# Turning the first attention's products round by head pairs, with attention weights turned by scaled identities

## The reference

```python
bias = jnp.full((n, n), NEG).at[diag, diag].set(0.0).at[dst, src].set(edge_weight)
q, k, v = jnp.split(x @ Wqkv.T + bqkv, 3, axis=-1)            # then 8 heads of 64 features
scores = jnp.einsum('hnd,hmd->hnm', q, k) / np.sqrt(HEAD_DIM) + bias[None]
attn = jax.nn.softmax(scores, axis=-1)
out = jnp.einsum('hnm,hmd->hnd', attn, v).transpose(1, 0, 2).reshape(n, EMBED_DIM)
h = layer_norm(x + out @ Wo.T + bo, g1, beta1)
h = layer_norm(h + (h @ W1.T + b1), g2, beta2)
```

## Time and profile before

| | us |
|---|---|
| median of three runs | 522.73 |
| profiled execution | 521.94 |
| its span | 519.9 |
| TensorE busy | 463.9 (89%) |
| VectorE busy | 323.7 (62%) |
| ScalarE busy | 181.5 (35%) |
| mean granted TensorE clock | 0.971 |

### The profile page before, as it was taken

The page is one execution under the profiler, slowest core; times in us unless marked ns, Lnnn a source line. Parts: engine busy times, 40 slices in busy tenths (PEclk is TensorE's granted clock), DMA queues, the critical chain, the costliest instruction groups (busy, mean ns, idle before and its releaser), DMA issues.

```text
span 519.9 us, 6791 instructions
## 1 busy us (share of the span) xinstructions
PE 463.9 (89%) x2153; PEld 274.4 (53%) x2153; DVE 323.7 (62%) x653; ACT 181.5 (35%) x352; POOL 151.0 (29%) x161
## 2 busy tenths in 40 slices
PE   6769999999689999998999999757898799998995
PEld 2422256665558998443444444545553587443442
DVE  7978989899968774787125200489998700267115
ACT  1259677665448762112101021242343232002010
POOL 5449034433350024132003500246633400003000
PEclk9988999999887999998999999899999999999998
DMA  7700000000044008152400020000002100000002
GB/s 256 264 2 0 1 1 2 2 1 2 2 149 177 1 2 314 57 196 82 141 0 0 5 77 0 0 1 0 1 1 90 73 1 0 1 0 0 0 1 81
DMA packets 13601, 25.80 MB, mean 50 GB/s; under 512 B 896, under 2 KB 1280, under 8 KB 13568
## 3 DMA queue, kind: packets, MB, share of 16 engines
q1 hardware_dynamic: 13568, 25.38, 14.1%
HBM read 24.33 MB, written 1.05 MB: 49 GB/s over the span
## 4 chain that ended last, share of the span: by engine, by line
PE 58%; DVE 32%; issue 4%; ACT 3%; DVEq 2%; DMA 0%; POOL 0%; POOLq 0%; SPq 0%; ACTq 0%
PE ring L1207 32%; PE banks L1376 5%; PE ring L1213 4%; DVE G L1158 4%; DVE G L1152 4%; DVE G L1169 4%; DVE HH L879 3%; PE ring L1476 3%; PE banks L1476 3%; PE banks L1316 2%; PE ring L1286 2%; DVE X L861 2%; DVE W_SD L905 2%; PE ring L1460 1%; DVE st L1024 1%
## 5 line engine op out<-in xcount | busy, mean ns | idle before, releaser
L1207 PE MATMUL ring<-G,WA 128*128 128x512 f32 x160 | 71.9, 605 | 3.1 <-ACT WA L562 2.5
L500 POOL TENSOR_TENSOR RB<-X,vec 128x512 f32<-128x512 f32 x16 | 21.1, 1328 | 148.1 <-DVE X L1049 110.1
L1207 PEld LDWEIGHTS ring<-G,WA 128*128 128x128 f32 x160 | 30.4, 194 | 39.5 <-issue 36.8
L470 POOL TENSOR_TENSOR A_SD<-A_SD,HH 128x128 f32 x64 | 32.0, 500 | 63.4 <-ACT HH L622 55.4
L1316 PE MATMUL banks<-RB,WB 128*128 128x128 f32 x256 | 45.6, 304 | 0.0
L1053 DVE TENSOR_TENSOR HH<-ring,RB 128x512 f32<-128x512 f32 x14 | 9.6, 686 | 53.1 <-PE ring L1207 53.1
L1152 DVE TENSOR_REDUCE G<-ring 128x256 f32<-128x2048 f32 x8 | 18.3, 2292 | 36.0 <-PE ring L1460 35.8
L576 ACT ACTIVATE sd<-mv,eps 128x1 f32<-128x1 f32 x32 | 9.4, 294 | 86.9 <-DVE mv L1029 86.9
L1316 PEld LDWEIGHTS banks<-RB,WB 128*128 128x128 f32 x256 | 37.1, 206 | 0.0
L562 ACT ACTIVATE WA<-ring 128x512 f32<-128x512 f32 x40 | 23.2, 591 | 35.6 <-PE ring L1213 35.6
L534 POOL TENSOR_TENSOR G<-G 128x1024 f32<-128x1024 f32 x7 | 16.5, 2358 | 59.9 <-ACT G L698 44.7
(11 more groups left out here) (195 smaller groups left out, 910.4 us busy)
## 6 DMA issues: line engine op xcount, KB each, us to landing
WA<-in_wqkv SPq DMA_DIRECT2D x2, 1024.0 KB, 8.5
WB<-in_wo SPq DMA_DIRECT2D x2, 1024.0 KB, 6.7
WC<-in_w SPq DMA_DIRECT2D x2, 1024.0 KB, 7.9
G<-in_w SPq DMA_DIRECT2D x1, 2048.0 KB, 10.4
G<-in_w SPq DMA_DIRECT2D x2, 1024.0 KB, 6.8
WA<-in_xT SPq DMA_DIRECT2D x4, 256.0 KB, 4.9
WA<-in_wqkv SPq DMA_DIRECT2D x4, 256.0 KB, 5.1
vec<-in_g SPq DMA_DIRECT2D x4, 256.0 KB, 7.9
```

The costliest lines, as they stand in the source:

```text
L470: pool.tensor_tensor(win, win, cnt_g[:, q, :, :], ALU.add).then_inc(group_added, 1)
L500: pool.tensor_tensor(out_, x_, vec[:, slot[vector], :], ALU.add).then_inc(resid_ready, 1)
L1207: last = nc.tensor.matmul(t[:, :], lhs(k), rhs_(k), start=(k == 0), stop=(k == n_k - 1))
```

## The change

- The products are turned round: the values (64 columns of one head) are the loaded tile, and the turned weights stream, 512 columns at once. The result is already turned, features by nodes. Two heads make a pair: one writes partitions 0 to 63 and the other partitions 64 to 127 of the same bank, so bank `j` holds heads 2j and 2j+1.
- The division by the row sums moves into the turning. Instead of `transpose`, an ordinary product streams a 128 by 128 diagonal matrix, which is the identity scaled by the inverse sums (`inverse_diag`, in `QB`). The diagonals of two heads fit. VectorE takes the inverse of the sums of a head and writes the diagonals of odd blocks, ScalarE those of even blocks, both in the turn before.
- Exponentials and row extremes run two heads ahead (`HEADS_AHEAD`), and `probsT` holds four heads.
- VectorE copies a finished pair to `outT` (in `W_SD`). The tile `OT` is gone. `Wo` is applied with the pairs as the outer loop: the four blocks are finished only in the last quarter.
- The load of `w12b` (1,024 KB, into `W_SD`) moves behind the last `WO`, and GpSimd's four residuals in `QB` behind the last `PT`.

```diff
+HEADS_AHEAD = 2
...
-    for b in range(NB):
-        add("OT", (b,), "A")
...
-        probsT = [XT, WA[:, 2, :, :]]
+        probsT = [XT, WA[:, 2, :, :], KB, HH]
+        outT = W_SD
+        inverse_diag = QB[:, 2:4, :].rearrange("p s (b n) -> p s b n", b=NB)
...
-            wait_full(sp, ("BD", NB - 1))
-            load("w12b", W_SD[:, :, :], blocks(a["w12"][:, D:2 * D]))
             wait_full(sp, ("PT", H - 1, NB - 1))
...
             load("wo2", WB[:, :, :], blocks(a["wo2"]))
+            load("w12b", W_SD[:, :, :], blocks(a["w12"][:, D:2 * D]))
...
+            wait_full(pool, ("PT", H - 1, NB - 1))
             for b in range(NB):
                 resid(QB[:, b, :], X[:, b, :], "be20")
...
+            def spread_inverse(h):                       # ScalarE
+                act.wait_ge(sums_inverted, NB + h)
+                if h >= 2:
+                    wait_full(act, ("PT", h - 2, NB - 1))
+                for b in range(0, NB, 2):
+                    act.activation(inverse_diag[:, h % 2, b, :], ident[:, :], ACT.Copy,
+                                   scale=inverse_sums[:, h * NB + b:h * NB + b + 1]).then_inc(diag_by_act, 1)
-            for b in range(NB):
-                exp0(0, b)
+            for h in range(HEADS_AHEAD):
+                for b in range(NB):
+                    exp0(h, b)
             for h in range(H):
                 for b in range(NB):
-                    if h + 1 < H:
-                        exp0(h + 1, b)
+                    if h + HEADS_AHEAD < H:
+                        exp0(h + HEADS_AHEAD, b)
                     if b % 2 == 0:
-                        if b == 0 and h >= 2:
-                            act.wait_ge(head_done, h - 1)
-                        turned(("PT", h, b), probsT[h % 2], b)
-            for b in range(NB):
-                turned(("OT", b), XT, b)
+                        if b == 0 and h % 2 == 0 and h >= 4:
+                            act.wait_ge(out_full, h // 2 - 1)
+                        turned(("PT", h, b), probsT[h % 4], b)
+                    if b == 2 and h + 1 < H:
+                        spread_inverse(h + 1)
...
+            for b in range(NB):                          # VectorE
+                row_least(1, b)
+                invert(slice(b, b + 1), b + 1, b + 1)
+                spread_block(0, b)
             for h in range(H):
                 for b in range(NB):
-                    if h + 1 < H:
-                        row_least(h + 1, b)
+                    if h + HEADS_AHEAD < H:
+                        row_least(h + HEADS_AHEAD, b)
...
+                    if b == 1 and h + 1 < H:
+                        spread_inverse(h + 1)
...
+                if h % 2 and h >= 5:
+                    take_pair(h // 2 - 2)
...
+            def turn_weights(h, b):                      # TensorE
+                pe.wait_ge(exp_done, h * NB + b + 1)
+                pe.wait_ge(*diag_at(h, b))
+                t = claim(("PT", h, b))
+                for k in range(NB):
+                    last = nc.tensor.matmul(t[:, k * P:(k + 1) * P], cols(probs, h * NB + b, k),
+                                            inverse_diag[:, h % 2, b, :], start=True, stop=True)
+                last.then_inc(ring_full, 1)
+            def pair_out(j):
+                ...
+                wait_emptied(pe, ("PT", 2 * j + 1, NB - 2))
+                wait_emptied(pe, ("PT", 2 * j + 1, NB - 1))
+                for m in range(NB):
+                    for i in range(2):
+                        h = 2 * j + i
+                        last = nc.tensor.matmul(bank[j][i * HD:(i + 1) * HD, :], VB[:, m, h * HD:(h + 1) * HD],
+                                                probsT[h % 4][:, m, :], start=(m == 0), stop=(m == NB - 1))
+                last.then_inc(out_full, 1)
+            for h in range(H):
+                for b in range(NB):
+                    turn_weights(h, b)
                 if 2 <= h < 2 + NB:
                     pe.wait_ge(count_built, 1)
                     turn(("AD", h - 2), lambda k: cols(A_SD, k, h - 2))
+                if h % 2 and h > 1:
+                    pair_out(h // 2 - 1)
+            pair_out(H // 2 - 1)
+            pe.wait_ge(loads["wo0"], 16)
+            for k in range(NB):
+                pe.wait_ge(out_taken, k + 1)
                 for b in range(NB):
+                    t = claim(("WO", b)) if k == 0 else bank_of(("WO", b))
+                    last = nc.tensor.matmul(t[:, :], cols(outT, k, b), WB[:, k, :], start=(k == 0), stop=(k == NB - 1))
+                    if k == NB - 1:
+                        last.then_inc(ring_full, 1)
```

More of the change, by code:

```diff
@@ L322, in gnn_program @@
         out_full = sem("out_full")
+        sums_inverted = sem("sums_inverted")
+        diag_by_dve = sem("diag_by_dve")
+        diag_by_act = sem("diag_by_act")
         head_done = sem("head_done")
@@ L971, in row_least, with invert, spread_block, spread_inverse @@
                                          accum_out=nmax[:, k:k + 1]).then_inc(row_max, 1)
+            def invert(columns, exps, count):
+                dve.wait_ge(exp_done, exps)
+                dve.reciprocal(inverse_sums[:, columns], row_sums[:, columns]).then_inc(sums_inverted, 1)
+                dve.wait_ge(sums_inverted, count)
+            def spread_block(h, b):
+                k = h * NB + b
+                dve.tensor_scalar(inverse_diag[:, h % 2, b, :], ident[:, :], inverse_sums[:, k:k + 1], None,
+                                  ALU.mult).then_inc(diag_by_dve, 1)
+            def spread_inverse(h):
+                invert(slice(h * NB, (h + 1) * NB), (h + 1) * NB, NB + h)
+                if h >= 2:
+                    wait_full(dve, ("PT", h - 2, NB - 1))
+                for b in range(1, NB, 2):
+                    spread_block(h, b)
+            def take_pair(j):
+                dve.wait_ge(out_full, j + 1)
+                dve.tensor_copy(outT[:, j, :], bank[j][:, :]).then_inc(out_taken, 1)
             wait_emptied(dve, ("S", H - 1, NB - 1))
@@ L1002, in _ @@
             link(dve.reciprocal(rc[:, 1, :], cnt_d[:, :]))
-            dve.wait_ge(exp_done, H * NB)
-            link(dve.reciprocal(inverse_sums[:, :], row_sums[:, :]))
-            by_row = inverse_sums[:, :].rearrange("p (h b) -> p b h", b=NB)
-            for b in range(NB):
-                dve.wait_ge(out_full, b + 1)
-                dve.tensor_tensor(HH[:, b, :].rearrange("p (h d) -> p h d", h=H),
-                                  bank[b][:, :].rearrange("p (h d) -> p h d", h=H),
-                                  by_row[:, b, :].rearrange("p (h d) -> p h d", d=1).broadcast_to([P, H, HD]),
-                                  ALU.mult).then_inc(out_taken, 1)
+            for j in range(H // 2 - 2, H // 2):
+                take_pair(j)
             n_stats = [0]
@@ L1154, in center @@
                 if 4 <= u < NU - 1:
-                    dve.wait_ge(head_done, H - 1 + u - 3)
+                    dve.wait_ge(head_done, u - 3)
                 if u == NU - 1:
@@ L1356, in _, with diag_at @@
                 turn(("BD", b), lambda k: cols(W_SD, k, b))
-            for h in range(H + 1):
-                if h < H:
-                    for b in range(NB):
-                        pe.wait_ge(exp_done, h * NB + b + 1)
-                        turn(("PT", h, b), lambda k: cols(probs, h * NB + b, k))
-                if h == 0:
-                    continue
+            def diag_at(h, b):
+                if h == 0:
+                    return diag_by_dve, b + 1
+                count = (h - 1) * 2 + b // 2 + 1
+                return (diag_by_dve, NB + count) if b % 2 else (diag_by_act, count)
+            def turn_weights(h, b):
[7 more added lines that the diff above has]
+            def pair_out(j):
+                if j == 0:
+                    pe.wait_ge(values_ready, NB)
+                wait_emptied(pe, ("PT", 2 * j + 1, NB - 2))
[9 more added lines that the diff above has]
+                    turn_weights(h, b)
                 if 2 <= h < 2 + NB:
```

26 lines of the change are left out of this document (3 added, 23 removed).

## The result

The changed kernel takes 534.49 us (median of 5 runs, 534.44 to 540.3), the kernel before 522.73 (5 runs, 519.71 to 524.37). The ratio is 1.0258, with a 95% interval of 1.0219 to 1.0298. It is slower by about 12 us. The forecast was 535, with a range of 530 to 541, and slower at 0.91.

A forecast was written before the change was run, and what follows sets the result against it. In this stretch TensorE's work was taken to bound the kernel, plus any new waits. Terms of 7.5, 4.1 and 1.7 summed to 13.3 us on the profiled 521.94, giving 535 us, range 530 to 541.

The forecast's parts named there:

- three large terms: `Wo` starting 7.5 us later, 4.1 more between `Wo` and `W1`, and 1.7 of slow clock: 13.3 us.
- Work: TensorE in the heads: dearer turnings 16.6 us more, products 14.0 less, result turnings 1.76 less; net 0.9 more.
- The 0.23: In a pair's products: 0.23 us on top of eight 512-column passes, for the change of array width.
- The late first turning: Head 0: TensorE's first turning waits for VectorE's first diagonal and starts at 156.6 instead of 152.86.
- The loop: Heads 1 to 3 and 5: a circle of waits through TensorE, VectorE and ScalarE spaces head starts 5.5 us apart.
- Behind the heads: From `Wo` to the first `W1` product: block 0 fills late, VectorE's rounds lose cover, 4.1 us later.
- The clock: In the `W1` products: one stretch of lowered TensorE clock after the new wait, 1.7 us (nothing to 3.4).
- The second: Pair products: the two halves run one after another, 3.44 us more per pair, 13.8 in all, 549 us; chance 5%.
- The first: Turning in the heads: costs no more than before, 0.44 us per block, giving back 11.4, 524 us; chance 7%.
- The third: Heads 1 to 3: the clock stays at 1.2 GHz, 3.8 us more, 539 us; chance 10%.

The follow-up runs named there:

- e3: Changed kernel turning by products with the plain identity, no diagonals made or waited for, division by row sums left out: 528.3 us.
- e4: Changed kernel with VectorE's and ScalarE's diagonals for the next head placed earlier in their lists, ahead of the copies: 532.47 us.
- e1: Changed kernel with `Wo` applied block by block again, the pairs as the inner loop: 529.53 us.
- e8: Kernel before with only the `Wo` loop turned inside out, so all four blocks finish in the last quarter: 528.33 us.
- e2: Changed kernel turning by transposes (4 passes a block), diagonals still made and waited for but unused, division left out: 534.0 us.
- e12: Changed kernel turning each block twice by transposes (8 passes), diagonals made and waited for, division left out: 537.25 us.
- e11: e2 with each pair multiplied one head earlier, division left out: 532.77 us.
- e5: Changed kernel with the edits of both e1 and e4: 525.89 us.
- e13: e9 with VectorE's two count sums moved behind its pair copies: 516.67 us, ratio 0.99 to the kernel before.
- e9: Changed kernel without diagonals: transposes one head ahead, pairs one head later, division on the finished pair, `Wo` block by block: 519.38 us.

## Why the prediction was right

Its sum stood because its three large terms were waits that could be read off lists and durations.

**Work.** "Net 0.9 more: nearly nothing" held in kind. The sum has a slip: three pairs at 3.67 and one at 3.44 are 14.45, not 14.2, so its own prices give 1.1. With the prices measured it is 0.7 less (32 blocks at 0.47 more are 15.0, products 28.2 less 14.2, and 1.76 less), and e3 gives 0.81 less. A turned block was 0.91 (3.64 for four), not 0.96: the price per pass is 0.114, the lower half of the range, where I took 0.12. The first pair is 3.59 (181.81 to 185.40), against 3.67. The 0.23 in that was no measure of a change of width: in the same rows the eight full-width passes take 1.99, 0.27 above eight times 0.2145, so it can be no more than the end of a group. What a change of width costs no run here shows by itself; a pair is 0.16 above eight passes of 0.429, and eight full-width passes with `W1` between two turnings are 0.11 above (218.81 to 222.35 in the kernel before). The Trainium skill's rule on loads, set against my row in the prediction (TensorE: Matmul & The Clock Gate, LDWEIGHTS), gave an estimate of 0.86; the measured 0.91 lies between that and the 0.96 I took, so neither was exact.

**The late first turning.** 3.7 later by the forecast, 3.6 by the trace, and for the forecast's reason, VectorE's first diagonal behind head 1's first `row_least`. e3, without diagonals, starts where the kernel before does.

**The loop.** Forecast 5.5, measured 5.69. The mis-sized link is the last: I took 0.28 for ScalarE's first diagonal, while from its start at 171.47 to TensorE's at 171.96 it is 0.49. Two diagonals start to end take 0.68, and the exponential behind them follows 0.58 later, so one costs 0.29 in the list; but TensorE, which waits for it, starts 0.20 later than that. What the 0.20 is made of no row shows. The other links came within 0.03 of what I took: 2.06 for the turned blocks, 0.61, 0.60, 0.73, 0.72, 0.48. e4 shows the mechanism: the same instructions earlier in both lists, and the wait ahead of head 2 is 0.33.

**Behind the heads.** Forecast 4.1, measured 4.66. VectorE was ready when I said: block 1's last operation (L1081) ends 18.7 behind `Wo`:

```profile
225.22 0.69 DVE L1091 TENSOR_TENSOR HH<-ring,RB 128x512 f32<-128x512 f32 x1 [10.75 <-PE ring L1437]
...
231.63 0.75 DVE L1081 SCALAR_TENSOR_TENSOR HH<-HH,rstd,vec 128x512 f32<-128x512 f32 x1
```

The first residual (L1091) comes 11.56 behind `Wo`, against 11.45 forecast, and 231.63 and 0.75 is 232.38, T+18.7. What I missed is that the turning of block 1 already meets the fallen clock: 0.90 up to the product, where I had 0.44. e1 and e8 show the term alone, in both directions.

**The clock.** Forecast 1.7, measured 1.5 in the `W1` products and that 0.46 in the turning ahead of them. It fell in the gap behind `Wo` and not in e1, where the gap is 0.25.

**The total.** The three terms measured 13.87 against 13.3. That the median came within 0.5 of 535 is in part luck: I took 13.3 for what measured 13.87, and the rest of the span gave 2 of these back in the medians.

**The rivals.** The second is refuted: a pair takes 3.59, both halves together. The first was not right, since a block costs 0.91; and e2 shows that its price was wrong as well. With transposes the clock stayed low and the gain was 3.5, not 11.4. I had priced it at a clock that those heads didn't have. The third, the low clock through heads 1 to 3, did not come with products, but did with transposes in e2. Its condition ("TensorE waits 30% of that time") was a real danger. That the doubled passes kept it away is argued from e2 and e12, one trace each.

## What to carry to other kernels

When a result that an engine makes for another is put into a list behind copies and exponentials of the head before, follow it once round through all lists: the length of that circle, and not any engine's load, can set the pace, as here, and moving the small instruction forward in its list is a cheap remedy (e4). A loop turned inside out so that all blocks finish at once takes away the cover of whatever is done per block behind it; the price is read from the first block's chain. Halving TensorE's passes in a stretch where it waits may only halve its clock, as in heads 1 to 3 of e2, so price such a saving at both levels.

## What the hardware showed that I had not expected

**Transposes and the clock.** e2 kept 1.2 GHz for 24 us, e11 for 14, with four transposes a block. With eight passes a block, products or transposes, it was over in less than 4 us in the changed kernel and in e12 (0.57 over the 4 us from 158 in both) and in about 7 in e1, e4 and e5, and the clock was back before 162 in all five. The Trainium skill (TensorE: Matmul & The Clock Gate, Part 4: PE-mode transpose) says that the full level does not engage in transpose mode. This case speaks against it: in e12 the clock rose and stayed at 1.00 with transposes alone. What was different in e2 was how much TensorE did, not its kind: 16 passes and then a wait of 3.56 before 165.30, where e12 had 32 and a wait of 2.57. That this is the cause is argued, not shown, since one list can give either clock. e2 and e11 left the low level at different heads. The kernel before was at 0.50 from 155 to 161, and e8, with the same list up to `Wo`, stayed at 1.00. e13 was at 0.50 from 156 to 162, and e9, with the same TensorE list there, stayed at 1.00. What decides it stays open.

**Small products half the array wide.** 64 passes that stream 128 columns took 3.71 in e13, 0.058 each, about half of the 0.114 of a full-width pass. At the rate of `Wo`'s passes (0.429 for 512 columns) 128 columns need 0.107, and 64 passes in a row 6.9, so the two halves run side by side here too. Spreading 32 columns of inverse sums over partitions thus cost under 4 us of TensorE (e9's wait aside), less than half of what the diagonals cost (8.49).
